# Softmax reciprocals for two steps at a time, and GpSimd's normalising one step later, in a pipelined cross-attention kernel

## What is computed

```
scores = jnp.einsum('bnqhd,bnkhd->bnhqk', qh, kh) * scale      # 8 heads, chunks of 64 positions
scores = scores + jnp.where(km[:, :, None, None, :] > 0, 0.0, NEG)
attn = jax.nn.softmax(scores, axis=-1)
out = jnp.einsum('bnhqk,bnkhd->bnqhd', attn, vh).reshape(N, T, C)
out = out @ W_out.T + b_out
out = out.transpose(0, 2, 1) * masks
```

## Time and profile before

| | |
|---|---|
| median of three runs | 6893.18 us |
| the profiled execution | 6878.53 us, span 6876.1 us |
| PE matmul busy | 5928.1 us (86%) |
| DVE busy | 6084.7 us (88%) |
| ACT busy | 4455.0 us (65%) |
| POOL busy | 4813.1 us (70%) |
| row reciprocals L1006 | 768 of 128 x 8 |
| POOL's normalising L780 | 768, 813.0 us busy, 544.0 us idle before |

### The profile page before, as it was taken

One profiled execution on the slowest core, in us unless ns is written; L12 is line 12 of the kernel. 1 busy time (PEld: TensorE's weight loads), 2 busy tenths in 40 slices (PEclk: granted clock), 3 DMA queues, 4 the chain that ended last, 5 costly groups with the idle time before them and its releaser, 6 DMA issues. The chain is left out here.

```text
span 6876.1 us, 226732 instructions
## 1 busy us (share of the span) xinstructions
PE 5928.1 (86%) x84308; PEld 3577.8 (52%) x84308; DVE 6084.7 (88%) x8460; ACT 4455.0 (65%) x17112; POOL 4813.1 (70%) x4750
## 2 busy tenths in 40 slices
PE   8888888888888888888888888888857949999999
PEld 4555555545454555455545555555532327767776
DVE  7999999999999999999999999999976578777876
ACT  6777777777777777777777777777741543333333
POOL 6788888888888888888888888888870013333332
PEclk9988988889888888888888888889868979999999
DMA  1222222222222222222222222222223003332322
GB/s 34 75 71 84 80 78 71 78 71 78 71 87 80 78 72 83 80 77 71 77 71 77 72 75 92 73 76 83 70 95 72 0 22 85 84 92 80 91 80 76
DMA packets 245853, 508.79 MB, mean 74 GB/s; under 512 B 155868, under 2 KB 169436, under 8 KB 210780
## 3 DMA queue, kind: packets, MB, share of 16 engines
q1 hardware_dynamic: 244700, 493.37, 22.7%
HBM read 377.93 MB, written 65.01 MB: 64 GB/s over the span
## 5 line engine op out<-in xcount | busy, mean ns | idle before, releaser
L653 ACT ACTIVATE prob<-SC,row_max 128x64 f32<-128x64 f32 x6144 | 1830.1, 325 | 1080.2 <-DVE row_max L998 1037.2
L769 POOL TENSOR_TENSOR k_bd<-k_t,head_mask 128x512 f32<-128x512 f32 x1536 | 1700.6, 1128 | 7.4 <-POOL dist_row L747 4.5
L653 ACT ACTIVATION_READ_ACCUMULATOR prob<-SC,row_max 128x1 f32 x6144 | 1336.8, 218 | 0.0
L982 DVE FIND_INDEX8 nbr<-top,dist 128x8 uint16<-128x1024 f32 x1024 | 1234.5, 1217 | 0.0
L978 DVE MAX8 top<-dist 128x8 f32<-128x1024 f32 x1024 | 1192.8, 1205 | 12.2 <-DVE y_b L1021 9.9
L780 POOL TENSOR_TENSOR prob<-prob,row_rec 128x512 f32<-128x512 f32 x768 | 813.0, 1059 | 544.0 <-DVE row_rec L1006 543.3
L553 PE MATMUL SC<-k_bd,q_t 128*64 128x256 f32 x6144 | 923.8, 426 | 0.0
L980 DVE MATCH_REPLACE8 dist<-top,dist 128x1024 f32<-128x1024 f32 x768 | 923.4, 1206 | 0.0
L561 PE MATMUL PT<-ident,prob 128*128 128x128 f32 x3072 | 543.7, 304 | 401.5 <-ACT prob_t L660 396.2
L1780 DVE TENSOR_TENSOR d_oh_a<-lo,iota_a 128x4096 bf16<-128x4096 bf16 x256 | 583.8, 2291 | 245.8 <-PE DM L1632 245.6
L1673 ACT ACTIVATE dense<-DM 128x512 f32<-128x512 f32 x512 | 305.4, 597 | 756.5 <-PE DM L1632 756.2
(11 more groups left out here) (201 smaller groups left out, 10825.7 us busy)
## 6 DMA issues: line engine op xcount, KB each, us to landing
low_all<-low_scratch SPq DMA_DIRECT2D x256, 1024.0 KB, 5.1
placed<-compact SPq DMA_DIRECT2D x256, 192.0 KB, 3.8
ctx<-in_ctx SPq DMA_DIRECT2D x32, 512.0 KB, 4.1
mask<-in_mask SPq DMA_DIRECT2D x32, 512.0 KB, 7.3
xb<-in_x SPq DMA_DIRECT2D x32, 512.0 KB, 4.8
x_scratch<-xb SPq DMA_DIRECT2D x32, 512.0 KB, 5.0
y_scratch<-y_b SPq DMA_DIRECT2D x32, 512.0 KB, 6.6
d_x<-x_scratch SPq DMA_DIRECT2D x32, 512.0 KB, 5.0
```

The costliest lines, as they stand in the source:

```text
L653: last = act.activation(prob[:, s % 4, g * CHUNK:(g + 1) * CHUNK], SC[:, s % 2, g * CHUNK:(g + 1) * CHUNK], ACT.Exp, bias=row_max[:, s % 2 ...
L769: last = pool.tensor_tensor(k_bd[:, q % KEY_BUFS, ch, :].rearrange("p (h k) -> p h k", h=8), kk, hm, ALU.mult)
L982: last = dve.max_index(nbr[:, uu % BPB, t, k * 8:(k + 1) * 8], best, row)
```

## The change

DVE takes the reciprocals of two pairs at once, at even steps only: at step s it waits for the exponentials of pair s - 1 and inverts the sums of pairs s - 2 and s - 1 in one instruction of 128 x 16. `LAG_SUM` becomes 2, so POOL normalises pair s - 2 at step s in place of pair s - 1. `LAG_T` stays 3: PE still transposes pair s - 3 at step s. `row_sum` and `row_rec` get four slots, and the waits count pairs of steps.

```diff
-LAG_SUM, LAG_T, LAG_PV, LAG_O, LAG_Y = 1, 3, 4, 5, 6
+LAG_SUM, LAG_T, LAG_PV, LAG_O, LAG_Y = 2, 3, 4, 5, 6
...
-        row_sum = sb("row_sum", [128, 2, 8])
-        row_rec = sb("row_rec", [128, 2, 8])
+        row_sum = sb("row_sum", [128, 4, 8])
+        row_rec = sb("row_rec", [128, 4, 8])
...
-                    act.wait_ge(recip_ready, at_least(i, START + i * STEPS + s - 1, START))
+                    act.wait_ge(recip_ready, at_least(i, START + i * (STEPS // 2) + s // 2 - 1, START))
                     for g in range(8):
                         last = act.activation(prob[:, s % 4, g * CHUNK:(g + 1) * CHUNK], SC[:, s % 2, g * CHUNK:(g + 1) * CHUNK], ACT.Exp,
-                                              bias=row_max[:, s % 2, g:g + 1], accum_out=row_sum[:, s % 2, g:g + 1])
+                                              bias=row_max[:, s % 2, g:g + 1], accum_out=row_sum[:, s % 4, g:g + 1])
...
                 if real(i, r, STEPS):
-                    pool.wait_ge(recip_ready, START + i * STEPS + r + 1)
+                    pool.wait_ge(recip_ready, START + i * (STEPS // 2) + r // 2 + 1)
                     pr = prob[:, r % 4, :].rearrange("p (h k) -> p h k", h=8)
-                    pool.tensor_tensor(pr, pr, row_rec[:, r % 2, :].unsqueeze(2).to_broadcast([128, 8, CHUNK]), ALU.mult).then_inc(normed, 1)
+                    pool.tensor_tensor(pr, pr, row_rec[:, r % 4, :].unsqueeze(2).to_broadcast([128, 8, CHUNK]), ALU.mult).then_inc(normed, 1)
...
                 r = s - LAG_SUM
-                if real(i, r, STEPS):
-                    dve.wait_ge(exped, START + i * STEPS + r + 1)
-                    dve.wait_ge(normed, at_least(i, START + i * STEPS + r - 1, START))
-                    dve.reciprocal(row_rec[:, r % 2, :], row_sum[:, r % 2, :]).then_inc(recip_ready, 1)
+                if real(i, r, STEPS) and r % 2 == 0:
+                    dve.wait_ge(exped, START + i * STEPS + r + 2)
+                    dve.wait_ge(normed, at_least(i, START + i * STEPS + r - 2, START))
+                    dve.reciprocal(row_rec[:, r % 4:r % 4 + 2, :], row_sum[:, r % 4:r % 4 + 2, :]).then_inc(recip_ready, 1)
```

## The result

The changed kernel takes 7007.36 us (median of 4 runs, 7004.63 to 7008.23) against 6893.77 (4 runs, 6890.46 to 6906.41): a ratio of 1.016, 95% interval [1.014, 1.018]. That is +114 us, where +60 was forecast. The direction and the range held. The profiled execution took 7007.35 us with a span of 7004.8. Against the profiled execution of before it is 129 us longer, and no offset between profile and median is left to carry over.

The account below looks back on a forecast made before the run. DVE was taken to set the attention stage's pace. 30 turns x 2.5 us = 75, less 15 for reciprocals, is +60: 6938 us from the profiled 6878.5, plus a 14.7 us offset, 6953 us; range 6895 to 7030.

Parts of the forecast that it names:

- The price of a reciprocal: DVE's queue: each reciprocal removed saves 0.11 us, and eight more elements in the remaining one cost 0.05 us.
- the -15 us term: DVE at steps 3 to 19: merged reciprocals save 0.48 us per batch element, -15 us for 32 elements.
- rival 2: Each removed reciprocal is worth its whole 189 ns and more steps count: 53 us saved; chance 0.06.
- That is worth nothing by itself: POOL's waits at odd steps go, but the gain is lost waiting for DVE at step 20.
- Step 23's late transposes: PE loses 3.4 us waiting for POOL; 2.36 us already spent waiting for `dist_row` swallows most of it.
- turn B: Second profiled passage from step 20 to the next element's step 3, 46.60 us before; forecast +1.5 us, nearly fixed by POOL.
- Step 0's transposes: PE waits for POOL's normalising ending at 2052.07; transposes begin at 2052.20, step 1's row maxima come 3.6 us late.
- turn A: First profiled passage from step 20 to the next element's step 3, 44.47 us before; forecast +3.5 us.
- the 5.44 us: Time from step 0's transposes to step 1's row maxima, taken over unchanged from the old profile.
- rival 3: PE at half clock through the turn: 5.5 us a turn, sum +150, 7043 us; chance 0.17.
- The mean of the two turns: Loss per turn between batch elements, averaged from two profiled turns: 2.5 us, due in 30 turns, 75 us.
- the main case: Late transposes cost 1.6 to 4 us a turn: 6893 + 33 to + 105 us; chance 0.68.

Follow-up runs that it names:

- e11: e9 with reciprocals merged two pairs at a time for pairs 4 to 17, seven instructions fewer per batch element; 6928.84 us, ratio 1.0043.
- e12: e9 with only POOL's wait edited: normalising an even pair from 4 to 16, it also waits for the next pair's reciprocal; 6927.28 us, ratio 1.0048.
- e1: Changed kernel with a separate reciprocal for every step again, POOL's normalising still one step later; 6910.99 us, ratio 1.003.
- e7: Changed kernel with spare PE products while it waits for the normalising, 12 at step 23 and 16 at step 0; 7055.26 us, ratio 1.023.
- e9: e1 with POOL's normalising at its old place from step 20 to step 3; 6859.25 us, ratio 0.995.

## Why the prediction was right, and where it was not

- **The price of a reciprocal** held: 384 of 128 x 16, 240 ns each, 0.16 us of the queue against 0.11 (forecast 0.11 + 0.05). The steps 3 to 19 gave back 0.27 us per element, where the -15 us term had 0.48. But that agreement is partly chance: single steps moved by up to 1.2 us either way (step 14 +1.19, step 15 -0.87). The clean test is e11 against e12, which differ in the merging and in ACT's matching wait alone. It saved 0.17 us an element, and the times of 6928.84 and 6927.28 do not tell them apart. (ACT waited 193 us for reciprocals in e11 and 39 in e12, over 1000 to 4800 us, which may have taken back a part.) So rival 2 is refuted in this kernel. The Trainium skill ("VectorE: DVE Perf Modes", on the errata) has every such instruction pay a fixed latency; by the prediction's estimate from its figure, 0.16 us an instruction, seven merged instructions an element would have saved 36 us.
- **"That is worth nothing by itself"**, on POOL's waits at odd steps, held for the change against the kernel before: POOL enters step 20 as it did (+1.57 us, before +1.72). But the sentence hid what the pairing takes. With single reciprocals the lag alone would have removed POOL's waits altogether and put it 3.8 us ahead (e1). The pair takes this back. I priced the pair by DVE's queue alone and never asked what its consumer loses by waiting for the second half. By the table 2.0 of the 4.68 us of the turn, and 1.3 us in the other steps, stand between e1 and the change: 30 x 2.0 + 32 x 1.3 = 102 us, where 96 were measured.
- **Step 23's late transposes** were to begin 3.4 us late with most of it swallowed. They did come late, by 3.2 us: a stop of 3.27 us. But the swallowing holds only for turns like A, where the wait for `dist_row` is gone. In turn B, of which the prediction read POOL's and DVE's rows and not PE's, the 3.25 us before the distances were the stop at the loop's jump, which follows PE and came again (3.52 us). There nothing was swallowed.
- **Step 0's transposes** were to begin at 2052.20 - 2021.53 = 30.67 us after the row maxima of step 20. Measured: 2098.17 - 2067.74 = 30.43. That POOL fixes this point was right to a quarter of a us in turn A. In turn B ("nearly fixed by POOL") it was wrong: 30.82 forecast, 31.54 measured, with no wait for POOL in front.
- **The step that failed in turn A is the 5.44 us** from there to step 1's row maxima, "as the clock then is likely to be as it was in the rows". Measured in turn A: 2105.38 - 2098.17 = 7.21, 1.77 more. The clock was at 0.52 for the 5.9 us behind the second stop; e7, which kept it at 1.00, took 4.54. This is the mechanism of rival 3, whose 5.5 us a turn stand nearer to the measured 4.68 than my 2.5; but it counted 3 us for the clock, and no turn showed so much. Over all 29 turns the way takes 6.59 us, 1.15 more than forecast; before the change it took 5.83, so turn A's 5.44 was itself a low value. The Trainium skill ("TensorE: Matmul & The Clock Gate", Part 1), which has the lower clock as the default and activity releasing it, spoke for the upper case. The granted clock behind both stops (0.57 and 0.52) agrees with it.
- **From step 1 to step 3** I had 11.89 us. It was 12.32, a further 0.43. Turn A in all: 48.00 forecast, 49.96 measured, made of -0.24, +1.77 and +0.43. Turn B: 3.76 us lost in place of 1.5 (50.36 against 46.60), of which the transposes of step 0 are 0.72 over the forecast, the way to step 1 1.07 and the rest 0.42.
- **The mean of the two turns.** I forecast 2.5 us and 4.68 were measured. Of the missing 2.15 us, 1.15 are the way from step 0's transposes to step 1, 0.33 the transposes themselves, 0.35 the steps 1 to 3, and 0.32 the choice of two turns whose mean before the change (45.54) lay above that of all (45.22). That the time still fell into the range is owed to its width, which took in a part of rival 3, and not to the main case: in part it was luck.
- **"This one costs nothing"**, on step 2's transposes, held in the changed kernel: there the transposes of step 2 do not wait in turns like A. In e7 that wait takes over as soon as the one before it shrinks.
- **"Nothing at steps 4 to 19 is waited for at an absolute time"** held, and the loss of a turn was not given back. The attention stage alone is longer: its last row maxima come 127 us later, and what follows them takes 1821 us in place of 1820.
- **DVE's idle time** in front of row maxima went from 24 x 161.3 / 574 = 6.74 to 24 x 244.2 / 560 = 10.47 us an element, +3.7 where 2 to 3 were forecast.
- **The offset of 14.7 us** between profile and median did not repeat (7007.35 against 7007.36). Without it the forecast would have been 6938, further off; it covered part of the error.

## What to carry to other kernels

Merging two small instructions into one delays whoever consumes the first half until the second half exists: price that wait on the consumer's engine, through its own queue, before counting the instruction saved. Where a step must move later on an engine that is sometimes ahead and sometimes behind, move it only where the engine is ahead (e9: one step later in the quiet part, the old place at the turn, 6859 us against 6911 for e1 and some 6894 before). Before a wait is booked as room that will swallow a delay, look at every kind of turn: a stop like the one at the loop's jump here comes again behind the delay. And when a change adds a stop of some us to PE, take the following products at the lower clock into the sum.

## What the runs showed of the hardware that was not expected

**DVE instructions last up to three times as long beside POOL's.** In e9 the two products `apart` and `r` start when POOL's work of the step is done:

```profile
2009.84 1.05 POOL L791 TENSOR_TENSOR prob<-prob,row_rec 128x512 f32<-128x512 f32 x1
```
```profile
2010.85 0.68 DVE L1087 TENSOR_TENSOR apart<-r2m,r 128x512 f32<-128x512 f32 x1
2011.45 0.68 DVE L1088 TENSOR_TENSOR r<-r,r2m 128x512 f32<-128x512 f32 x1
```

In e12 the same two run beside the `k_bd` products and the normalising. Both are slower, and so is the normalising, but not the `k_bd` products (2.04 us for two):

```profile
2042.51 2.04 POOL L770 TENSOR_TENSOR k_bd<-k_t,head_mask 128x512 f32<-128x512 f32 x2 [0.16 <-POOL dist_row L748]
2044.51 1.49 POOL L791 TENSOR_TENSOR prob<-prob,row_rec 128x512 f32<-128x512 f32 x1
```
```profile
2043.82 1.28 DVE L1087 TENSOR_TENSOR apart<-r2m,r 128x512 f32<-128x512 f32 x1
2045.03 1.53 DVE L1088 TENSOR_TENSOR r<-r,r2m 128x512 f32<-128x512 f32 x1
2046.48 0.68 DVE L1010 TENSOR_REDUCE row_max<-SC 128x8 f32<-128x512 f32 x1
```

The product `r` takes 1.53 us in place of 0.68, and the normalising 1.49 in place of 1.05. The one-input `r2m` goes from 0.45 to 1.37 in the mean. Row maxima, which read PSUM, stay at 0.68 us in every kernel. The Trainium skill ("GPSIMD Engine Reference", Key points) says that GpSimd contends with DVE instructions that have two SBUF inputs or run in a two-port mode. The rows agree with the first kind; no run here tells in which mode `r2m` ran. A schedule that shifts POOL thus changes single groups of DVE's instructions by 0.5 to 2 us a batch element, up or down. In e12 these changes nearly cancelled (+0.17 us), so their sum has to be looked at before a single one is made the cause.

**Behind the same stop the lower clock can set in at once or later.** In turn A, behind its stop of 3.27 us, PE's transposes still ran at the full rate (0.66 us), and the two distance products 2.6 us later took 1.91. The stop of step 23 is 2.9 to 3.3 us long in all 29 turns; in 18 of them the transposes behind it took 0.66 to 0.74 us and in 11 they took 1.11 or 1.12. Behind the stop of 3.43 us they were slow at once (1.12). After the spare products of e7 a stop of 1.00 us was followed by a clock of 1.00.
